# Attention on one core: q and k of one head in one projection, spread by DMAs, and another order of the work beside the softmax

## The reference

```
qkv = einsum('bse,ehd->bshd', xn, w_qkv)      # 16 heads, q, k, v of 64 each
logits = q k^T / 8, causal mask               # float32
out = einsum('bshd,hde->bse', softmax(logits) v, w_out)
```

## Time and profile before

| | before |
|---|---|
| median of 3 runs (lowest, highest) | 3604.49 us (3602.31, 3604.86) |
| the profiled execution: time, span | 3601.74 us, 3599.9 us |
| mean granted TensorE clock | 0.981 |
| PE, DVE, ACT, POOL busy | 3330.4, 2229.2, 2091.6, 1442.9 us |
| PE, DVE, ACT, POOL share of the span | 93%, 62%, 58%, 40% |

### The profile page before, as it was taken

One profiled execution on the slowest core, in us unless ns is written; L12 is line 12 of the kernel. 1 busy time (PEld: TensorE's weight loads), 2 busy tenths in 40 slices (PEclk: granted clock), 3 DMA queues, 4 the chain that ended last, 5 costly groups with the idle time before them and its releaser, 6 DMA issues.

```text
span 3599.9 us, 66241 instructions
## 1 busy us (share of the span) xinstructions
PE 3330.4 (93%) x23060; PEld 2752.3 (76%) x23061; DVE 2229.2 (62%) x5743; ACT 2091.6 (58%) x4500; POOL 1442.9 (40%) x2023
## 2 busy tenths in 40 slices
PE   4599999999799999999999999999999999999997
PEld 3489989999677777777777777777777777777775
DVE  6744444443366666666666666666666666666666
ACT  3354544444366666666666666666666666666664
POOL 2222222220233345444444444454444444445445
PEclk7799999999899999999999999999999999999999
DMA  6112222221311111212212122111222212211111
GB/s 210 42 44 72 73 71 71 72 68 33 96 39 39 51 49 48 52 48 60 55 49 52 48 57 56 48 52 48 55 55 53 52 48 53 56 51 45 42 39 53
DMA packets 177498, 207.65 MB, mean 58 GB/s; under 512 B 50144, under 2 KB 150560, under 8 KB 177184
## 3 DMA queue, kind: packets, MB, share of 16 engines
q1 hardware_dynamic: 164896, 169.96, 17.0%
q0 software_dynamic: 12288, 33.57, 3.4%
HBM read 102.80 MB, written 33.55 MB: 38 GB/s over the span
## 4 chain that ended last, share of the span: by engine, by line
PE 63%; DVE 5%; ACT 4%; issue 1%; POOL 1%; ACTq 0%
PE S L1168 17%; PE T L1180 14%; PE O L1198 12%; PE S L1090 7%; PE S L1105 3%; PE W L1105 3%; PE S L1123 3%; PE W L1123 2%; DVE kk L1321 2%; PE W L1090 2%; ACT kk L1258 2%; ACT pr L1240 2%; DVE res L1311 1%; DVE S L1351 1%; POOL ql L1449 0%
## 5 line engine op out<-in xcount | busy, mean ns | idle before, releaser
L1428 POOL TENSOR_SCALAR pr<-pr,rinv 128x128 f32<-128x128 f32 (+7 forms) x1024 | 767.9, 751 | 1351.4 <-DVE rinv L1290 1348.8
L1240 ACT ACTIVATE pr<-S,negm 128x128 f32<-128x128 f32 (+7 forms) x1024 | 759.9, 742 | 625.8 <-DVE negm L1351 518.6
L1351 DVE CUSTOM_DVE_ANT_0 S<-S,late 128x128 f32<-128x128 f32 (+7 forms) x1024 | 778.1, 760 | 134.8 <-PE S L1168 132.7
L1168 PE MATMUL S<-kk,qh 128*128 128x256 f32 (+2 forms) x1536 | 607.1, 395 | 140.4 <-ACT pr L1240 140.4
L1180 PE MATMUL T<-ident,pr 128*128 128x128 f32 x4608 | 687.4, 274 | 14.1 <-POOL pr L1428 12.0
L1180 PEld LDWEIGHTS T<-ident,pr 128*128 128x128 f32 x4608 | 543.6, 141 | 84.6 <-DVE pT L1228 16.7
L1198 PE MATMUL O<-pT,vv 128*64 128x256 f32 (+1 forms) x5120 | 585.4, 367 | 0.1
L1228 ACT ACTIVATE pT<-T 128x512 f32<-128x512 f32 (+3 forms) x768 | 415.4, 541 | 183.7 <-PE T L1180 176.2
L1168 PE MATMUL S<-kk,ql 128*128 128x256 f32 (+2 forms) x1536 | 515.6, 343 | 0.0
L1168 PEld LDWEIGHTS S<-kk,qh 128*128 128x128 f32 x1536 | 288.4, 188 | 284.1 <-ACT pr L1240 184.1
L1198 PEld LDWEIGHTS O<-pT,vv 128*64 128x64 f32 x5120 | 334.9, 137 | 200.1 <-issue 47.1
(11 more groups left out here) (186 smaller groups left out, 6329.5 us busy)
## 6 DMA issues: line engine op xcount, KB each, us to landing
qh<-qh SPq DMA_DIRECT2D x128, 256.0 KB, 3.7
ql<-ql SPq DMA_DIRECT2D x128, 256.0 KB, 4.7
y<-yb SPq DMA_DIRECT2D x128, 128.0 KB, 1.7
wr<-in_L_attn_w_qkv SPq DMA_DIRECT2D x128, 128.0 KB, 2.3
x<-in_L_attn_x SPq DMA_DIRECT2D x16, 512.0 KB, 5.2
xn<-xn SPq DMA_DIRECT2D x16, 512.0 KB, 5.3
w1r<-in_L_ffn_w SPq DMA_DIRECT2D x8, 1024.0 KB, 5.1
w2r<-in_L_ffn_w SPq DMA_DIRECT2D x8, 1024.0 KB, 8.1
```

What stands on the lines that cost most here:

```text
L1168: ins = e.matmul(S[s % 2][:, a:b], t[q][h][:, i * P:(i + 1) * P], kk[q][h][:, a - off:b - off], start=(t is qh), stop=(t is ql))
L1240: e.activation(pr[i][:, 0:w], S[s % 2][:, off:off + w], ACT.Exp, bias=negm[:, i:i + 1], scale=-1.0, accum_out=rsum[:, i:i + 1]).then_inc(e ...
L1351: e.tensor_tensor_reduce(masked, masked, late[:, SEQ - w:], 1.0, -MASKED, ALU.add, ALU.min, negm[:, i:i + 1]).then_inc(negmax.sem, 1)
L1428: e.tensor_scalar(pr[i][:, 0:width(s)], pr[i][:, 0:width(s)], rinv[:, i:i + 1], 1.0, ALU.mult, ALU.mult).then_inc(scaled.sem, 1)
```

## The change

- A projection's 128 rows are now q and k of one head (`p0`, `p1` for head 0 and token halves 0 and 1, `p2`, `p3` for head 1). The weights lie so in `wh` and `wl`, and q's weights are scaled by -1/8 on POOL before they are split.
- A piece is drained by one ACT copy on all 128 partitions (high parts of q and k, to `qq`) and one DVE subtraction (low parts, to `kk`). `qh` is now called `qq`.
- SP's `spread` takes the place of `double`: four DMAs a head. It waits for the head's second piece, copies the low part of q to both halves of `ql`, waits, copies the high part of k to the upper half of `kk`, waits, and copies the high part of q over k in `qq`. Scores of steps 0 and 1 wait for the spread of their head.
- `STEP_OF`, `BANK_OF` and `AFTER` are new: the four projections at steps 1, 2, 4 and 6 instead of 0, 1, 1 and 2, xn at 0, v0 and v1 at 6 and 8, o3 at 10, o0 at 11; the groups at 10, 11, 15 and 16, 19 and 20. `split_w` comes at step 7 instead of 3.
- The ring of `pr` has 6 tiles instead of 4.
- `last_sum` comes two a step from step 12 of the last unit.

```
-    STEPS, LAG, RING = 2 * QT, 3, 4
+    STEPS, LAG, RING = 2 * QT, 3, 6
-    STEP_OF = {"q0": 0, "q1": 1, "k0": 1, "k1": 2, "o2": 2, "xn": 4, "v0": 5, "v1": 7, "o3": 7, "o0": 9, "o1": 13}
-    BANK_OF = {"q0": 0, "q1": 1, "k0": 2, "k1": 0, "o2": 1, "xn": 2, "v0": 0, "o3": 1, "v1": 2, "o0": 2, "o1": 2,
-               "v2": 0, "v3": 1}
+    STEP_OF = {'xn': 0, 'p0': 1, 'o2': 2, 'p1': 2, 'p2': 4, 'p3': 6, 'v0': 6, 'v1': 8, 'o3': 10, 'o0': 11, 'o1': 13}
+    BANK_OF = {'p0': 2, 'p1': 0, 'p2': 2, 'p3': 2, 'o2': 1, 'xn': 0, 'v0': 1, 'o3': 2, 'v1': 2, 'o0': 2, 'o1': 2, 'v2': 0, 'v3': 1}
-        AFTER = [4 * g + 3 + LAG + 1 + (g == GROUPS - 1) for g in range(GROUPS)]
+        AFTER = [10, 11, 15, 19]
...
-            def double(n):
-                e.wait_ge(act.sem, act.at(n, "q1"))
-                e.wait_ge(dve.sem, dve.at(n, "q1"))
-                q = (n + 1) % 2
-                for t in (qh, ql):
-                    e.dma_start(t[q][0][HDIM:P, :].bitcast(F32), t[q][0][0:HDIM, :].bitcast(F32)).then_inc(dup.sem, 16)
-                    e.dma_start(t[q][1][0:HDIM, :].bitcast(F32), t[q][1][HDIM:P, :].bitcast(F32)).then_inc(dup.sem, 16)
+            def spread(n, h):
+                to, up, down = (n + 1) % 2, slice(0, HDIM), slice(HDIM, P)
+                q_, l_, k_ = (t[to][h] for t in (qq, ql, kk))
+                e.wait_ge(act.sem, act.at(n, f"p{2 * h + 1}"))
+                e.wait_ge(dve.sem, dve.at(n, f"p{2 * h + 1}"))
+                e.dma_start(l_[up, :].bitcast(F32), k_[up, :].bitcast(F32)).then_inc(moved[h].sem, 16)
+                e.dma_start(l_[down, :].bitcast(F32), k_[up, :].bitcast(F32)).then_inc(moved[h].sem, 16)
+                e.wait_ge(moved[h].sem, moved[h].at(n + 1, 32))
+                e.dma_start(k_[up, :].bitcast(F32), q_[down, :].bitcast(F32)).then_inc(moved[h].sem, 16)
+                e.wait_ge(moved[h].sem, moved[h].at(n + 1, 48))
+                e.dma_start(q_[down, :].bitcast(F32), q_[up, :].bitcast(F32)).then_inc(moved[h].sem, 16)
...
-                if s == 0:
-                    e.wait_ge(dup.sem, dup.at(n, 64))
-                    e.wait_ge(act.sem, act.at(n - 1, "k1"))
-                    e.wait_ge(dve.sem, dve.at(n - 1, "k1"))
+                if s < 2:
+                    e.wait_ge(moved[h].sem, moved[h].at(n, 64))
...
-                    cols = slice(int(name[1]) * HALF, (int(name[1]) + 1) * HALF)
-                    dst, scale = (qh, -QSCALE) if name[0] == "q" else (kk, 1.0)
-                    for h in range(2):
-                        hs = slice(h * HDIM, (h + 1) * HDIM)
-                        ins = e.activation(dst[(n + 1) % 2][h][hs, cols], W[hs, :], ACT.Copy, scale=scale)
+                    h, f = int(name[1]) // 2, int(name[1]) % 2
+                    ins = e.activation(qq[(n + 1) % 2][h][:, f * HALF:(f + 1) * HALF], W, ACT.Copy)
...
-                    for h in range(2):
-                        hs, other = slice(h * HDIM, (h + 1) * HDIM), slice((1 - h) * HDIM, (2 - h) * HDIM)
-                        if name[0] == "q":
-                            ins = e.scalar_tensor_tensor(ql[to][h][hs, cols], W[hs, :], -QSCALE,
-                                                         qh[to][h][hs, cols].bitcast(F32), ALU.mult, ALU.subtract)
-                        else:
-                            ins = e.tensor_tensor(kk[to][h][other, cols], W[hs, :],
-                                                  kk[to][h][hs, cols].bitcast(F32), ALU.subtract)
+                    h, f = int(name[1]) // 2, int(name[1]) % 2
+                    cols = slice(f * HALF, (f + 1) * HALF)
+                    ins = e.tensor_tensor(kk[(n + 1) % 2][h][:, cols], W, qq[(n + 1) % 2][h][:, cols].bitcast(F32), ALU.subtract)
...
-                if n == UNITS - 1 and s >= STEPS // 2:
-                    last_sum(s - STEPS // 2)
+                if n == UNITS - 1 and s >= STEPS - HT:
+                    last_sum(2 * (s - STEPS + HT))
+                    last_sum(2 * (s - STEPS + HT) + 1)
...
-                for c_ in range(MC):
-                    e.tensor_scalar(put(wh, c_), raw_qk(c_), 1.0, 1.0, ALU.mult, ALU.mult).then_inc(whi.sem, 1)
-                e.wait_ge(whi.sem, whi.at(m, MC))
-                for c_ in range(MC):
-                    e.tensor_tensor(put(wl, c_), raw_qk(c_), put(wh, c_).bitcast(F32), ALU.subtract).then_inc(wlo.sem, 1)
+                e.tensor_scalar(raw_q, raw_q, -QSCALE, 1.0, ALU.mult, ALU.mult).then_inc(wscaled.sem, 1)
+                e.wait_ge(wscaled.sem, wscaled.at(m, 1))
+                e.wait_ge(filled.sem, filled.at(m - 1, "p3"))
+                e.tensor_scalar(wh[:], wr[:], 1.0, 1.0, ALU.mult, ALU.mult).then_inc(whi.sem, 1)
+                e.wait_ge(whi.sem, whi.at(m, 1))
+                e.tensor_tensor(wl[:], wr[:], wh[:].bitcast(F32), ALU.subtract).then_inc(wlo.sem, 1)
...
-                if s == STEP_OF["k1"] + 1 and n + 2 < UNITS:
+                if s == STEP_OF["p3"] + 1 and n + 2 < UNITS:
                     split_w(n + 1)
```

More of the change, by code:

```diff
@@ L834, in attention_and_sum @@
     CHUNKS = FIRST_CH[STEPS]
-    assert all(FIRST_CH[4 * g] % 2 == 0 for g in range(GROUPS + 1)) and STEPS % RING == 0
-    STEP_OF = {"q0": 0, "q1": 1, "k0": 1, "k1": 2, "o2": 2, "xn": 4, "v0": 5, "v1": 7, "o3": 7, "o0": 9, "o1": 13}
-    BANK_OF = {"q0": 0, "q1": 1, "k0": 2, "k1": 0, "o2": 1, "xn": 2, "v0": 0, "o3": 1, "v1": 2, "o0": 2, "o1": 2,
-               "v2": 0, "v3": 1}
+    assert all(FIRST_CH[4 * g] % 2 == 0 for g in range(GROUPS + 1))
+    STEP_OF = {'xn': 0, 'p0': 1, 'o2': 2, 'p1': 2, 'p2': 4, 'p3': 6, 'v0': 6, 'v1': 8, 'o3': 10, 'o0': 11, 'o1': 13}
+    BANK_OF = {'p0': 2, 'p1': 0, 'p2': 2, 'p3': 2, 'o2': 1, 'xn': 0, 'v0': 1, 'o3': 2, 'v1': 2, 'o0': 2, 'o1': 2, 'v2': 0, 'v3': 1}
     SHORT = 2 * HT
-    BEFORE = ["q0", "q1", "k0", "k1", "v0", "v1", "v2", "v3"]
-    BY_ACT = {"q0", "q1", "k0", "k1", "xn", "v0", "v1", "v2", "v3"}
-    BY_DVE = {"q0", "q1", "k0", "k1", "xn", "o0", "o1", "o2", "o3"}
+    BEFORE = ["p0", "p1", "p2", "p3", "v0", "v1", "v2", "v3"]
+    BY_ACT = {"p0", "p1", "p2", "p3", "xn", "v0", "v1", "v2", "v3"}
+    BY_DVE = {"p0", "p1", "p2", "p3", "xn", "o0", "o1", "o2", "o3"}
     def pieces(n):
@@ L869, in attention_and_sum @@
         two = lambda f: [f(i) for i in range(2)]
-        qh, ql = (two(lambda i: two(lambda h: sb(f"q{n}{i}{h}", [P, SEQ], F32R))) for n in "hl")
-        kk = two(lambda i: two(lambda h: sb(f"kk{i}{h}", [P, SEQ], F32R)))
+        qq, ql, kk = (two(lambda i: two(lambda h: sb(f"{n}{i}{h}", [P, SEQ], F32R))) for n in ("qq", "ql", "kk"))
         vv = two(lambda i: sb(f"vv{i}", [P, QT, VW]))
@@ L882, in attention_and_sum @@
         xnt = sb("xnt", [P, MODEL])
-        wr = sb("wr", [P, MC, 2, 2 * HDIM])
-        wh, wl = (sb(f"w{n}", [P, MC, 2, 2, HDIM], F32R) for n in "hl")
+        wr = sb("wr", [P, MC * 2, 2 * HDIM])
+        wh, wl = (sb(f"w{n}", [P, MC * 2, 2 * HDIM], F32R) for n in "hl")
         wvr = sb("wvr", [P, MC, 4, HDIM])
@@ L990, in attention_and_sum @@
         dve = Pieces(sem("s_dve"), BY_DVE)
-        dup = Count(sem("s_dup"), 64)
+        moved = two(lambda h: Count(sem(f"s_moved{h}"), 64))
         wload, wvload = Count(sem("s_wload_a"), 32), Count(sem("s_wvload"), 32)
-        whi, wlo = Count(sem("s_whi_a"), MC), Count(sem("s_wlo_a"), MC)
+        wscaled, whi, wlo = (Count(sem(f"s_{n}_a"), 1) for n in ("wscaled", "whi", "wlo"))
         wvhi, wvlo = Count(sem("s_wvhi"), MC), Count(sem("s_wvlo"), MC)
@@ L1020, in group_at @@
             return None
-        spare = [t[0][h][:, i * MODEL:(i + 1) * MODEL].bitcast(F32) for t in (qh, ql) for h in range(2) for i in range(SEQ // MODEL)]
+        spare = [t[0][h][:, i * MODEL:(i + 1) * MODEL].bitcast(F32) for t in (qq, ql) for h in range(2) for i in range(SEQ // MODEL)]
         last_y = [spare[j * QT:(j + 1) * QT] for j in range(TOPK)]
@@ L1026, in attention_and_sum @@
         ALL = [(n, s) for n in range(UNITS) for s in range(STEPS)]
-        END = [(UNITS, s) for s in range(LAG + GROUPS + 1)]
+        END = [(UNITS, s) for s in range(12)]
         @block.sync
@@ L1037, in load_wv @@
                     e.dma_start(wvr[:, c_], wvv[m % (PAIRS // 2)][:, c_, :, 2 * HDIM:]).then_inc(wvload.sem, 16)
[L1039 to L1045 removed]
+            def spread(n, h):
[9 more added lines that the diff above has]
+                e.dma_start(q_[down, :].bitcast(F32), q_[up, :].bitcast(F32)).then_inc(moved[h].sem, 16)
             load_w(1)
             load_wv(1)
[L1049 to L1050 removed]
+            for h in range(2):
+                spread(-1, h)
+            e.wait_ge(wlo.sem, wlo.at(0, 1))
             load_w(2)
@@ L1057, in _ @@
                 if n + 1 < UNITS:
-                    double(n)
+                    for h in range(2):
+                        spread(n, h)
                 if n + 3 < UNITS:
-                    e.wait_ge(wlo.sem, wlo.at(n + 1, MC))
+                    e.wait_ge(wlo.sem, wlo.at(n + 1, 1))
                     load_w(n + 3)
```

(4 more changed lines are left out.)

43 lines of the change are left out of this document (21 added, 22 removed).

## The result

The changed kernel takes 3426.39 us (median of 4 runs, 3424.01 to 3431.05) against 3603.5 us of the kernel before on the same chip: ratio 0.951, interval 0.9494 to 0.9526. The mechanism was the forecast one and the gain was 177 us instead of 125.

What follows compares the result with a forecast made beforehand. The attention stage was taken as bound by PE work plus its waits for ScalarE's exponential. From 3601.7 us, minus 132.7 (loop), plus 5 (start) and 2 (end) gave 3476.0, or 3479 us at the median; range 3462 to 3545.

Steps and rivals of the forecast that it cites:

- the first term: Attention loop: PE's waits at steps 4 and 5, 2.14 us a unit, vanish in 62 units, gaining 132.7 us.
- The sum of the old order: PE's work in one attention unit, read off the chain of waits: 38.8 us plus the waits; new order 38.9 us.
- The copies: Spreading DMAs in the loop: three stages of 4.5 us, 13.5 to 14.5 with issues, within 21 us; no cost.
- the ring: Six pr tiles free ACT from transposes of four steps ago, which PE does before the awaited scores anyway: nothing.
- POOL's cover: Step 8's scaling waits behind the weight split, its transposes some 4 us later: no cost; under 1 us a unit if uncovered.
- The end: Last unit: DVE's last sums, two a step in steps 12 to 15, cost +2 us, between 0 and 3.
- Steps 10 and 11 are the tight ones: DVE drains o3, group 0, o0, group 1 there; o0 has 0.2 to 0.4 us in hand; no wait priced.
- The start: Before unit 0 nothing covers the copy chain; PE stands some 9 us; cost +5 us, between 2 and 10.
- more is gained: Rival, chance 0.08: the start costs nothing, stages are short and value groups begin sooner: 3465 us.
- Small waits: Rival, chance 0.20: small waits at steps 10 and 11 replace two large ones, 0.6 us a unit: 3516 us.
- The stall only moves: Rival, chance 0.05: the exponential stays 2.1 us late somewhere in each unit, nothing gained: 3611 us.
- Late spread: Rival, chance 0.05: head 1's copies delay scores 1, deciding from 7 us a stage; +425 us at 10 us a stage.

Runs made afterwards that it cites:

- The run with nearly empty drains: The kernel before, order and instructions kept, but drains of q and k take 64 of 512 columns from unit 1 on: 3451.75 us, ratio 0.9572.
- the run with the work first: The changed kernel with the piece of work done before the transposes, not between transposes and values, at steps 4, 10 and 11: 3448.71 us, ratio 0.957.
- v1 at step 8: The changed kernel with the old order of steps, banks and groups, and v1 moved from step 7 to 8: 3615.6 us, ratio 1.0034 to the kernel before.

## Why the prediction was wrong

**The step that failed** is the first term, "62 units of 2.14 are 132.7 us", with "the question is the waits" read from rows of PE's idle time. The mechanism was right: the drains held up the exponentials of steps 2 and 3, and with them gone the scores of steps 4 and 5 wait for nothing. The term was mis-sized: it measured 185.0 us. The run with nearly empty drains shows why for 2.48 us of each unit: there 2.14 us of marked waits were worth 2.48. The other 0.51 us stood at steps 7 to 11 of the old order, of which the prediction said that "the only two waits of a unit are those of steps 4 and 5". PE's rows show none there; the weight loads' rows show about half of it.

The reason lies in how the rows are made. A matmul of 128 columns is drawn 0.27 us long, while the next one starts 0.11 us after it. Idle time counts from the end as drawn, so the row of each stall behind transposes is short by up to 0.16 us, and one below that has no row; the lists leave out gaps under 0.15 us besides. The sum of the old order, "38.8 and the waits", carried what the rows leave out inside the pieces of the chain, and so it went into the 38.9 us of the new order too (its sixteen terms add to 39.0). By the changed kernel's chain the excess is spread over steps 4, 5, 6, 8, 10 and 11, 0.13 to 0.19 us each. Two of its causes can be read: step 6's scores were taken at 0.67 us, behind values, and are 0.47 behind transposes; step 10's at 0.86, behind o0 and perhaps part stall, and are 0.71. With 38.9 for 38.0 the two errors were one and the same, and the sum looked closed.

The Trainium skill (Trainium Kernel Development and Optimization, Performance Expectations) calls matmul busy time a bad metric of how close a kernel is to its limit (the roofline), because matmuls are pipelined, and the weight loads' busy share a good one. The traces agree: with the same matmuls PE's busy time fell from 3330.4 to 3285.3 us, so some 45 us of it had been no work, while the weight loads' went from 2752.3 to 2747.4.

**What held.** One drain on 128 partitions costs what one on 64 did: 597 and 692 ns. The copies are hidden; a stage is 2.8 to 3.6 us, shorter than the bounds of the rows taken from four in flight. POOL and the ring cost nothing; POOL's cover is thin, 0.28 us a unit when it goes. The end cost 2.1 us for 2. Steps 10 and 11 are the tight ones: o0's one step of room is needed, as the run with the work first shows, but there is no wait in them.

**What was off besides.** The start cost 2.9 us instead of 5: the wait of about 9 us came (10.1 us, for xn, whose load stands behind both heads' copies), but v0 no longer waits 2.89 us (p3 waits 1.50), and the copies were shorter. The slow matmuls there came as forecast. The prediction calls those of the earlier trace rows doubled; as drawn they are 0.69 us for 0.44, and what halved is the granted clock, here in the kernel before just behind the wait of 3.78 us (it was 1.00 from 961.2 to 965.0):

```profile
971.70:973.50 1.80, 1.65 (x5) 1.15 (x5) 0.72 (x2) 1.30 (x3) 0.00 (x0) 0.50 0.98 275
```

The range's upper side was the wider one, for new waits; the lower side held only 17 us for a gain left out of the sum. The case "more is gained" had the right sign and neither its mechanism nor its size.

**The rivals.** Small waits: none in the loop. The stall only moves: no; but it takes little to bring it back, as v1 at step 8 did with +158 us. Late spread: not here, with 11.9 us in hand for a forecast of 6.5; before it decides, the xn load behind it on SP does, from 7 us of delay.

## What to carry to other kernels

Before pricing a stall on PE, take the time lost from the starts of instructions, step against like step, and not from the gaps between a drawn end and a start. The waits of the weight loads, read beside those of the matmuls, point to stalls that the matmuls' rows hide; here they came within 0.1 us a unit of the loss in three kernels and missed most of it in two others (0.17 of 1.27, none of 0.4). In a loop whose queues work in order, moves of one piece by one step are worth tens of microseconds in either direction; check for each what shares its PSUM bank, what it stands in front of, and what it covered where it was. And when two edits attack the same backlog (here 100 and 148 us alone, 177 together), their gains don't add.

## What the runs showed of the hardware

- A wait of PE of 4.2 us, once a unit, costs more than itself: the granted clock was 0.50 in the 3.5 us behind it (1.2 GHz, of 2.4), and eight value matmuls took 1.48 us instead of 0.80.
- A change between float32r and float32 matmuls looks like 0.09 us in the starts (0.21 us from the first to the second matmul of a value piece, 0.12 between the next ones), yet removing two of them at step 4 gained 0.04 us in all.
- A drain of 512 columns takes the same time on 128 partitions as on 64: 597 and 590 ns on ACT, 692 and 689 ns on DVE.
- A 128-column transpose is drawn 0.27 us long and the next starts 0.11 us after it, so the profile's idle time behind transposes is short by up to 0.16 us.
- Copies of 256 KB between partitions of SBUF land in 2.8 us when one is in flight, and in 3.6 for the second of two issued together.
- Profiled executions reached the attention's first projection up to 9.5 us apart (942.95 to 952.42) after the same instructions.
